# Result tiles of the last unit one by one, scatters that wait per tile and per expert, a second block of padding rows

## The reference

```python
def _dispatch_compute(xf, top_expert, w1, w2, capacity):
    ...
    tok_idx = indices[jnp.minimum(pos, tokens - 1)]
    xe = jnp.where(valid[..., None], xf[tok_idx], 0.0)
    h = jax.nn.gelu(jnp.einsum('ech,ehf->ecf', xe, w1), approximate=True)
    ye = jnp.einsum('ecf,efh->ech', h, w2)
    tok_safe = jnp.where(valid, tok_idx, tokens)
    out = jnp.zeros((tokens + 1, hs), xf.dtype).at[tok_safe.reshape(-1)].add(ye.reshape(-1, hs))
    return out[:tokens]
...
for k in range(TOPK):
    y = _dispatch_compute(xf, top_experts[:, k].astype(jnp.int32), w1, w2, capacity)
    out = out + y * expert_weights[:, k][:, None]
h = h + out + bias
```

## Time and profile before

| | us |
|---|---|
| timed runs (three) | 716.57, 717.54, 721.19 |
| their median | 717.54 |
| the profiled execution's own time | 715.48 |
| its span, first to last record | 713.6 |
| TensorE busy in the span | 647.0 (91%) |
| ScalarE busy | 378.1 (53%) |
| VectorE busy | 401.1 (56%) |
| GpSimd busy | 303.8 (43%) |

### The profile page before, as it was taken

How to read it: one execution, slowest core, us unless ns; L and a number is a source line. 1 busy time by engine, 2 the same in 40 slices (tenths; PEclk the granted TensorE clock), 3 DMA queues, 4 the chain that set the end, 5 groups by cost and what they waited for, 6 DMA issues and landing times. The chain is left out here.

```text
span 713.6 us, 14553 instructions
## 1 busy us (share of the span) xinstructions
PE 647.0 (91%) x5574; PEld 543.9 (76%) x5574; DVE 401.1 (56%) x1005; ACT 378.1 (53%) x800; POOL 303.8 (43%) x401
## 2 busy tenths in 40 slices
PE   2797999989899898999989869999999999999992
PEld 2555666666667666667767869999999999999992
DVE  4886685777867687648765144444444444444320
ACT  4365766747567485565661065545554444555540
POOL 3300001003121131030423659877788888888233
PEclk9999999999999998999999979999999999999997
DMA  7448392604333043153102252444444444442223
GB/s 256 112 117 227 89 271 69 198 32 137 106 83 113 9 113 90 44 151 128 63 24 76 76 202 66 104 104 104 105 104 105 104 104 104 105 104 46 24 29 37
DMA packets 66477, 73.76 MB, mean 103 GB/s; under 512 B 6312, under 2 KB 61458, under 8 KB 66408
## 3 DMA queue, kind: packets, MB, share of 16 engines
q1 hardware_dynamic: 55584, 59.27, 27.6%
q0 software_dynamic: 9504, 13.00, 10.7%
q10 hardware_dynamic: 1320, 0.57, 0.3%
HBM read 31.62 MB, written 22.35 MB: 76 GB/s over the span
## 5 line engine op out<-in xcount | busy, mean ns | idle before, releaser
L1588 DVE TENSOR_TENSOR hl<-h,hh 128x384 fp32r<-128x384 f32 x128 | 103.8, 812 | 155.2 <-ACT h L1545 155.2
L1081 DVE TENSOR_REDUCE mx<-s_bank 128x2 f32<-128x256 f32 (+2 forms) x192 | 124.4, 684 | 56.6 <-PE s_bank L580 55.5
L1542 ACT ACTIVATE hh<-t_bank 128x384 fp32r<-128x384 f32 x128 | 63.0, 492 | 132.5 <-PE t_bank L1630 130.2
L889 ACT ACTIVATE pt<-t_bank 128x512 f32<-128x512 f32 x128 | 76.5, 598 | 68.0 <-PE t_bank L602 65.4
L1511 POOL DMA_INDIRECT out<-yo,xr x48 | 75.1, 1564 | 71.3 <-ACT yo L1553 61.6
L1499 POOL TENSOR_TENSOR wl<-wr,wh 128x256 fp32r<-128x256 f32 x112 | 94.2, 875 | 1.2
L1630 PE MATMUL t_bank<-xh,wh 128*128 128x384 f32 x256 | 86.6, 338 | 0.0
L601 PE MATMUL t_bank<-qs,ks 98*128 98x384 bf16 (+2 forms) x384 | 85.7, 275 | 0.6 <-ACT pt L887 0.4
L1630 PE MATMUL t_bank<-xl,wh 128*128 128x384 f32 x256 | 86.2, 337 | 0.0
L1630 PE MATMUL t_bank<-xh,wl 128*128 128x384 f32 x256 | 86.0, 336 | 0.0
L579 PE MATMUL s_bank<-ks,qs 96*128 96x128 bf16 (+2 forms) x384 | 78.7, 274 | 5.0 <-DVE mx L1081 4.0
(11 more groups left out here) (191 smaller groups left out, 1451.8 us busy)
## 6 DMA issues: line engine op xcount, KB each, us to landing
wr<-in_w SPq DMA_DIRECT2D x16, 1024.0 KB, 5.8
qs<-part SPq DMA_DIRECT2D x96, 96.0 KB
ks<-part SPq DMA_DIRECT2D x90, 96.0 KB
slot_rows<-empty SPq DMA_DIRECT2D x4, 1560.0 KB, 9.1
xr<-slot_rows SPq DMA_DIRECT2D x16, 390.0 KB, 3.3
wr<-in_x SPq DMA_DIRECT2D x8, 768.0 KB, 5.6
out<-hid SPq DMA_DIRECT2D x8, 384.0 KB, 3.5
qs<-mT ACTq DMA_DIRECT2D x64, 3.0 KB
```

The lines of the kernel that those rows point to most:

```text
L889: ins = act.activation(pt[:, p, unit // 2, 0:AT[1]], bank, ACT.Exp)
L1081: ins = dve.tensor_reduce(mx[:, p // 2, j, 2 * (p % 2):2 * (p % 2) + 2], pair_region(s_bank, j), AX_X, ALU.max)
L1542: act.activation(hh[:, f, :], h_banks[f % NH], ACT.Gelu_apprx_tanh)
L1588: dve.tensor_tensor(hl[:, f, :], h[f % 2][:, :], hh[:, f, :].bitcast(F32), ALU.subtract).then_inc(hl_done, 1)
```

## The change

On TensorE the last unit's results are computed tile by tile: `result` takes the tiles that it is to do, and behind the interleaved loop, which now ends with unit 14, a loop over the tiles goes outside and the one over f inside. The scatters of GpSimd wait for their own tile each. The semaphore `added` becomes two, one for each k; a unit of k = 0 still waits for all scatters of all units before, while a unit of k = 1 waits only for those of the experts before, and not for the unit of k = 0 of its own expert. Since the places that no token takes would let these two units add to the same padding rows, the padding is now two blocks of 128 rows, one for each k, and `empty` and the column of row numbers are doubled.

```diff
-OUT_ROWS = TOKENS + P
+OUT_ROWS = TOKENS + TOPK * P
...
-        token = buf("token", [P, TILES + 1], I32)
-        empty = buf("empty", [P, 1, ROW])
+        token = buf("token", [P, TILES + TOPK], I32)
+        empty = buf("empty", [P, TOPK, ROW])
...
-                    sp.dma_start(out[TOKENS:OUT_ROWS, :], empty[:, 0, 0:DIM]).then_inc(zeroed, 16)
-                share = SLOTS // P // PIECES
+                    sp.dma_start(out[TOKENS:OUT_ROWS, :].rearrange("(k p) d -> p k d", p=P),
+                                 empty[:, :, 0:DIM]).then_inc(zeroed, 16)
+                share, k = SLOTS // P // PIECES, i * TOPK // PIECES
                 flat = slot_rows.rearrange("(a p) d -> p a d", p=P)
                 sp.dma_start(flat[:, i * share:(i + 1) * share, :],
-                             empty[:, :, :].to_broadcast([P, share, ROW])).then_inc(zeroed, 16)
+                             empty[:, k:k + 1, :].to_broadcast([P, share, ROW])).then_inc(zeroed, 16)
...
-            pool.tensor_copy(empty[:, 0, DIM:DIM + 1].bitcast(I32), token[:, TILES:TILES + 1]).then_inc(empty_made, 1)
+            pool.tensor_copy(empty[:, :, DIM].bitcast(I32), token[:, TILES:TILES + TOPK]).then_inc(empty_made, 1)
...
-        added = sem("added")
+        added = [sem(f"added{k}") for k in range(TOPK)]
...
-                    sp.wait_ge(added, 16 * CT * (u + 1))
+                    sp.wait_ge(added[u % TOPK], 16 * CT * (u // TOPK + 1))
...
             def add_rows(u):
 
-                pool.wait_ge(y_sb, CT * (u + 1))
-                if u:
-                    pool.wait_ge(added, 16 * CT * u)
-                else:
+
+                for k in range(TOPK if u >= TOPK else 0):
+                    pool.wait_ge(added[k], 16 * CT * (u // TOPK))
+                if u == 0:
                     pool.wait_ge(res_out, 16 * B)
                 for t in range(CT):
+                    pool.wait_ge(y_sb, CT * u + t + 1)
                     pool.indirect_dma_start(
...
-                        compute_op=ALU.add).then_inc(added, 16)
+                        compute_op=ALU.add).then_inc(added[u % TOPK], 16)
...
-            pool.wait_ge(added, 16 * CT * U)
+            for k in range(TOPK):
+                pool.wait_ge(added[k], 16 * CT * E)
...
-                    act.wait_ge(added, 16 * CT * (u - 1))
+                    act.wait_ge(added[k], 16 * CT * (u // TOPK))
...
-            def result(u, f):
+            def result(u, f, tiles=range(CT)):
...
-                for t in range(CT):
+                for t in tiles:
...
-            for u in range(U):
+            for u in range(U - 1):
                 for f in range(FC):
                     result(u, f)
-                    if u + 1 < U:
-                        hidden(u + 1, f)
+                    hidden(u + 1, f)
                     if u + 2 < U and f == ROWS_AT:
                         transpose_rows(u + 2)
+            for t in range(CT):
+                for f in range(FC):
+                    result(U - 1, f, (t,))
```

More of the change, by code:

```diff
@@ L464, in _ @@
             pool.memset(empty[:, :, :], 0.0).then_inc(empty_made, 1)
-            pool.iota(token[:, :], pattern=[[P, TILES + 1]], base=0, channel_multiplier=1).then_inc(empty_made, 1)
+            pool.iota(token[:, :], pattern=[[P, TILES + TOPK]], base=0, channel_multiplier=1).then_inc(empty_made, 1)
             pool.wait_ge(empty_made, 2)
-            pool.tensor_copy(empty[:, 0, DIM:DIM + 1].bitcast(I32), token[:, TILES:TILES + 1]).then_inc(empty_made, 1)
+            pool.tensor_copy(empty[:, :, DIM].bitcast(I32), token[:, TILES:TILES + TOPK]).then_inc(empty_made, 1)
             pool.wait_ge(empty_made, 3)
```

## The result

The changed kernel takes 713.64 us (median of 20 runs, 710.52 to 717.54), the kernel before in the same runs 717.28 us (20 runs, 714.33 to 721.19). The ratio is 0.9952, with a 95% interval from 0.9936 to 0.9968: 3.4 us less, between 2.3 and 4.6. The prediction said 713.8 us and 3.7 us less. In the later runs of the experiments the kernel before took 728.9, 733.4 and 727.8 us (medians of three sets), so each kernel there is compared with the runs of before in its own set.

The account below looks back on a forecast made before the run. TensorE bounds the expert stage; behind its last matmul, two scatter slots on GpSimd were to go, 3.7 us, all else zero: median 717.54 less 3.7 gives 713.8 us, range 711.8 to 717.5.

Parts of the forecast that it names:

- TensorE doesn't wait for the rest: Expert stage, 431 to 690 us: TensorE busy 259.00 of 259.00 us, so only its work or what follows can move the end.
- The order of the results: Last unit on TensorE: tile by tile, stride stays 0.12 us, tiles scaled at about 695.16, 698.03 and 700.90; extra checks free.
- The room at f = 7 of tile 0: Last unit: VectorE's low half ends at 693.20, TensorE needs it at 694.05; 0.85 us left, costed at zero.
- The waits: GpSimd's last two units: scatters wait per tile and per expert, so the last starts at 701.69 instead of 705.40, 3.71 us earlier.
- the lower of the two bounds: Gap between GpSimd's scatters behind a satisfied wait: 0.30 us taken, giving 3.71; at 0.78 the gain would be 2.13.
- Neither part alone: End of the last unit: tile order alone gains zero; with all of unit 14 to be landed first, the gain is 1.76 us.
- The page's rule: Skill's rule at the last scatters: issued almost together, so no gain, 717.5 us; within the no-gain rival, chance 0.05.
- The closing: After the last scatter lands: 4.4 us until the span's end, assumed to follow that landing.
- The padding and GpSimd's extra waits: First and expert stages: larger padding store at most 0.5 us, longer GpSimd gaps 0.96 covered by 2.67 idle; both costed zero.

Follow-up runs that it names:

- e7: Changed kernel with three spare VectorE subtractions ahead of the very last low half; last scatter 10.84 us behind the last unit's first result matmul, against 10.08 in the changed kernel.
- e2: Changed kernel with the last unit's results interleaved again, so only waits and padding changed; ratio to the kernel before 1.0012, whole end 13.0 us.
- e10: Changed kernel with tiles 0 and 1 of the last unit interleaved, then tile 2; one run, last scatter 2.21 us behind TensorE's last matmul, whole end 10.4.
- e1: Kernel before with only the last unit's results computed tile by tile on TensorE; ratio to the kernel before 0.9988, whole end 13.5 us.
- e3: Changed kernel where a k = 1 unit again waits for its expert's k = 0 unit to land; ratio to the kernel before 0.9984, whole end 12.1 us.
- e5: Kernel before without the scatters of tiles 1 and 2 of the last unit; 729.37 against 733.37 us, ratio 0.9943.
- e8: Kernel before with the last unit's scatters sending 64 of their 128 rows each; a scatter holds GpSimd 1.43 us instead of 1.55.
- e6: Kernel before without any scatter of the last unit; span 723.3 us, closing 4.15 us behind ScalarE's end.
- e4: Kernel before with only the second padding block and wider `empty`; ratio to the kernel before 1.0022, whole end 13.5 us.
- e9: Changed kernel once more, unaltered, as a control in the last set of runs; 724.83 against 727.83 us for the kernel before, ratio 0.9959.

## Why the prediction was right

- **TensorE doesn't wait for the rest.** 255.00 of 255.00 us busy, as said. All that moved lies behind the last matmul.
- **The order of the results.** Predicted: the stride stays 0.12 us, ScalarE's scalings 2.9 apart. Measured: (699.59 - 691.08) / 71 = 0.12, and scalings at 694.21, 697.03, 699.90, that is 2.82 and 2.87 apart. The 16 more checks cost nothing. The room at f = 7 of tile 0 was put at 0.85 us; e7 measured 0.80.
- **The waits.** The six scatters were predicted at 0.09, 1.95, 3.81, 5.67, 7.53 and 10.16 us behind the first result matmul; they start at 0.19, 2.05, 3.91, 5.77, 7.62 and 10.08. The gap behind a satisfied wait is 0.30, the lower of the two bounds. The first is 0.1 late: its release took 0.87 us (scaled at 690.40, start 691.27) where I had 0.78; the first scatters of e2 and e10 also take 0.87 and 0.86. It was swallowed ahead of the last scatter, which had 0.60 us of slack (0.90 idle less the gap of 0.30). The last is 0.08 early: I kept tile 2's scaling where it was, but it used to queue behind the other two, 0.39 us behind the start of its last matmul (700.43 - 700.04), and now it starts after 0.31. Hence 3.79 us and not 3.71.
- **Neither part alone.** Predicted: tile order alone nothing, everything except the per-expert wait 1.76 us. Measured: 0.1 (e1) and 1.6 (e3). The waits alone, which the prediction didn't price, give 0.6 (e2), so 3.8 is no sum of the parts: 0.1 + 0.6 = 0.7.
- **The page's rule.** That issuing costs almost nothing would have made the gain zero. The scatters start 1.86 us apart wherever only GpSimd holds them, and without two of them the last one starts 3.7 us sooner (e5). The Trainium skill, "DMA: Bandwidth & Descriptors", in the section on the anatomy of one DMA, calls descriptor generation small and says that many descriptors can be emitted before the added cost shows. For these indirect, adding scatters the trace doesn't bear out the first, if GpSimd's 1.55 us are that generation, which no row shows. It agrees with the second: 64 rows more cost 0.12 us (e8). The prediction took both for one rule.
- **The closing.** 4.4 us, assumed to follow the last landing: it does, since the end from the last scatter on is 8.1 to 8.3 us in every kernel with whole scatters, wherever that scatter stands. Where nothing landed later, it followed ScalarE, with 4.15 us (e6).
- **The padding and GpSimd's extra waits.** Zero in both, by e4 and by TensorE's busy time. In the middle units the first scatter starts 1.36 us behind ScalarE's first scaling (498.67 - 497.31) where it was 1.99 (499.76 - 497.77), so 0.63 us earlier and not 0.75, and GpSimd's idle time before it is 2.56 us against 2.67.

One effect was not foreseen: the pattern of VectorE's low halves changes. In the six kernels whose scatters wait in the old way their median is 0.64 to 0.71 us and the longest take 1.9 to 2.0; in the six with a wait for each tile (e2 and e3 among them) the median is 0.56 and the longest take 3.0 to 3.1, so that the next one is late. Their mean is no measure of this: it is 812 ns before, 857 in the changed kernel and 808 in e9, the same kernel once more. Low halves longer than 0.56 us stand beside GpSimd's weight splits, which the earlier scatters have moved; that this is the reason is argued from the times at which both run, and was not tried. TensorE waits for none of them (no idle time up to the last unit), so it costs nothing here. From the lists of the costliest groups of the changed kernel and of e9:

```profile
L1591 DVE TENSOR_TENSOR hl<-h,hh 128x384 fp32r<-128x384 f32 x128 | 109.0, 857 | 150.8 <-ACT h L1548 150.7
...
L1591 DVE TENSOR_TENSOR hl<-h,hh 128x384 fp32r<-128x384 f32 x128 | 102.7, 808 | 157.6 <-ACT h L1548 157.6
```

The absolute time fits better than it deserves. The difference of the medians is 3.64 us; that the prediction is only 0.2 us off is in part luck: it rests on the median of three runs of before (717.54) lying close to that of twenty (717.28).

## What to carry to other kernels

When a kernel ends in a row of transfers from one engine, look at how far apart they start: each slot behind the last result is paid in full, and it can be moved under the matmuls only if the results get ready one after the other and the waits let each go by itself. Both are needed, and a wait that was hidden in the old order can be the next bound in the new one. For gains of half a per cent, measure lengths inside the trace from a common event, since here they repeat to 0.1 us where the runs of one kernel lie 7 to 13 us apart.

## What the runs showed of the hardware

**An indirect scatter has a large fixed cost on GpSimd.** 1.55 us for 128 rows of 1 KB, 1.43 for 64, plus 0.30 to the next, also with a satisfied wait in between, and 0.8 to 0.9 us from the end of the scaling that it waits for to its start. The data move only once the issue is over. In the view of the transfers of before from 700 to 713 us (40 slices of 0.325 us, the share of the 16 DMA engines in tenths), the first scatter, issued from 701.69 to 703.24, shows from the 12th slice on, that is from 703.6 us. The other two, issued until 705.09 and 706.95, show from 705.5 and 707.5:

```profile
DMA  0000000000059971097960098940000000000000
```

**The same kernel differs from execution to execution ahead of the expert stage, along with TensorE's granted clock.** Beside e1 to e4, 35 executions of the kernel before had spans from 722.4 us at a mean granted clock of 0.978 to 734.9 us at 0.955. Over its runs and those of e1, a line through span and clock has a slope of 0.52 us for each 0.001 and leaves 0.7 us of scatter; with the clock taken out in this way, e1 is 0.1 +- 0.5 us longer than the kernel before and e4 0.1 +- 0.4 shorter. (TensorE is idle in the end, and its granted clock is low there, 0.67 from 700 to 713 us in the kernel before. So a shorter end shifts the mean clock too, and the line isn't used for such kernels.) The changed kernel's two profiles, spans 709.4 and 729.3, differ before the expert stage begins. The transfer that opens it, from the chain of waits of the first and of e9:

```profile
410.36 3.19 DMA xr<-slot_rows
```

```profile
429.73 3.15 DMA xr<-slot_rows
```

and the stretch from 200 to 300 us in both, where the clock (last column but two) is lower in the second:

```profile
200.00:300.00 100.00, 93.08 (x837) 64.73 (x836) 73.09 (x231) 62.78 (x130) 19.98 (x22) 0.97 0.27 78
```

```profile
200.00:300.00 100.00, 92.47 (x833) 63.98 (x831) 71.03 (x224) 60.41 (x126) 19.94 (x22) 0.93 0.26 73
```

Of 19.9 us between the spans, 19.4 are there already at the start of the expert stage. The lower clock and the longer stage come together; which of them causes the other, these runs don't tell.
